# Writing the destination one-hots with the tile index innermost, and loading them with that step

## What is computed

```python
def step(f, _):
    msg = f[src] * edge_weight[:, None]
    agg = jax.ops.segment_sum(msg, dst, num_segments=n)
    f = (1.0 - ALPHA) * agg + ALPHA * feat_0
    return (f, None)
out, _ = jax.lax.scan(step, feat, None, length=K)     # K = 10
```

## Time and profile before

| | us |
|---|---|
| median of 3 runs (8633.08 to 8642.26) | 8638.01 |
| the profiled execution's own span | 8640.6 |
| packing loop, in that span | about 1241 to 1745 |
| the ten hops | about 1750 to 5410 |
| the two single hops | in 7600 to 8640 |

### The profile page before, as it was taken

The page is one execution under the profiler, slowest core; times in us unless marked ns, Lnnn a source line. Parts: engine busy times, 40 slices in busy tenths (PEclk is TensorE's granted clock), DMA queues, the critical chain, the costliest instruction groups (busy, mean ns, idle before and its releaser), DMA issues. The chain is left out here.

```text
span 8640.6 us, 563982 instructions
## 1 busy us (share of the span) xinstructions
PE 7490.3 (87%) x228719; PEld 6386.0 (74%) x228719; DVE 6536.9 (76%) x13039; ACT 4071.0 (47%) x9117; POOL 5548.3 (64%) x5894
## 2 busy tenths in 40 slices
PE   4967758889999999999999999499999899949794
PEld 4856648889999999999999999344444454449794
DVE  5779979978888898888888888544444444478787
ACT  1229969944444444444444444244444444424242
POOL 2520000068888888888888888477777777738384
PEclk7559975589999999999999999799999999979797
DMA  5210026689999999999999999433333333249495
GB/s 80 92 47 0 0 69 246 247 299 342 338 338 339 340 340 336 340 340 338 340 340 338 339 338 339 122 77 79 78 79 79 79 79 77 64 161 339 161 338 166
DMA packets 833483, 1832.18 MB, mean 212 GB/s; under 512 B 245310, under 2 KB 306774, under 8 KB 831838
## 3 DMA queue, kind: packets, MB, share of 16 engines
q1 hardware_dynamic: 752974, 1777.08, 58.4%
q0 software_dynamic: 59776, 46.03, 4.8%
q10 hardware_dynamic: 20624, 7.81, 0.5%
HBM read 1667.67 MB, written 157.79 MB: 211 GB/s over the span
## 5 line engine op out<-in xcount | busy, mean ns | idle before, releaser
L1491 PE MATMUL banks<-arena 128*128 128x48 bf16 x58800 | 2352.6, 184 | 5.4 <-issue 5.4
L1491 PEld LDWEIGHTS banks<-arena 128*128 128x128 fp8e4 x58800 | 2270.5, 95 | 5.9 <-issue 5.7
L1457 DVE TENSOR_TENSOR banks<-banks,wslot 128x384 f32<-128x384 f32 (+1 forms) x3600 | 1984.5, 569 | 343.8 <-PE banks L1491 309.8
L1391 POOL TENSOR_TENSOR arena<-arena 128x768 bf16<-128x768 f32 (+2 forms) x1200 | 1838.3, 1540 | 422.6 <-DVE arena L1461 414.1
L1323 ACT CAST arena<-banks 128x384 bf16<-128x384 f32 (+1 forms) x2400 | 1178.8, 493 | 1872.6 <-DVE banks L1457 1693.7
L1491 PE MATMUL banks<-xc,arena 128*128 128x48 bf16 x24500 | 1943.0, 184 | 62.0 <-DVEq L1470 14.9
L1491 PEld LDWEIGHTS banks<-xc,arena 128*128 128x128 fp8e4 x24500 | 1864.4, 95 | 164.5 <-issue 104.7
L1773 POOL DMA_INDIRECT f<-node_table,idx x1568 | 1554.2, 991 | 557.6 <-issue 466.9
L1461 DVE TENSOR_TENSOR arena<-banks,arena 128x384 f32<-128x384 f32 (+1 forms) x2400 | 1350.4, 574 | 95.4 <-ACT arena L1323 2.3
L1505 PE MATMUL banks<-arena 32*128 32x144 bf16 x80400 | 1374.8, 222 | 21.5 <-issue 13.3
L1505 PEld LDWEIGHTS banks<-arena 32*128 32x128 bf16 x80400 | 1261.2, 93 | 49.2 <-issue 17.8
(11 more groups left out here) (385 smaller groups left out, 13650.6 us busy)
## 6 DMA issues: line engine op xcount, KB each, us to landing
arena<-onehots SPq DMA_DIRECT2D x1200, 512.0 KB, 4.9
arena<-onehots SPq DMA_DIRECT2D x1500, 256.0 KB, 5.2
arena<-onehots SPq DMA_DIRECT2D x300, 576.0 KB, 5.8
arena<-onehots SPq DMA_DIRECT2D x300, 544.0 KB, 5.3
arena<-in_dst SPq DMA_DIRECT2D x195, 512.0 KB
arena<-onehots SPq DMA_DIRECT2D x300, 288.0 KB
onehots<-arena SPq DMA_DIRECT2D x100, 768.0 KB, 3.2
arena<-key_rows SPq DMA_DIRECT2D x196, 196.0 KB
```

What stands on the lines that cost most here:

```text
L1391: nc.gpsimd.tensor_tensor(mp_low[b], mp_rest[b], mp_mid[b], ALU.subtract).then_inc(lo_done[b], 1)
L1457: nc.vector.tensor_tensor(bank, bank, w, ALU.mult).then_inc(m_done, 1)
L1491: m = nc.tensor.matmul(to, g_ring[b][:, i * P:(i + 1) * P], x_part, start=c == 0, stop=c == 2)
```

## The change

The scatter part of all six batches is now made by DVE with the same helper as the source part, so that it stands as `[e, t]`, tiles side by side. ScalarE's Abs and Relu instructions, GpSimd's key copy and their semaphores are gone; ScalarE keeps the fp8 copies. SP sends the same bytes from the same places, in the same order. In the hops the same bytes are loaded, and the ring's scatter part is read as `[e, t]`: a tile's 128 weight columns are 16, 17 or 18 bf16 elements apart (32 to 36 bytes), where they were adjacent.

```diff
-            ACT_B = NBATCH - 1
-            key_now = part(28700, NTILE[ACT_B])
-            far = part(23800, NTILE[ACT_B] * P // 2, BF16)
...
-            def by_tile_outer(to, keys):
-                shape = [P, keys.shape[1], P]
-                return nc.vector.tensor_tensor(to.rearrange("p (t e) -> p t e", e=P), iota_b[:, 0:P].unsqueeze(1).broadcast_to(shape),
-                                               keys.unsqueeze(2).broadcast_to(shape), ALU.is_equal)
-
             def s_part(b):
-                return packed[:, BATCH_AT[b] + G_COLS[b]:BATCH_AT[b] + BATCH_COLS[b]].bitcast(BF16)
+                return packed[:, BATCH_AT[b] + G_COLS[b]:BATCH_AT[b] + BATCH_COLS[b]].bitcast(BF16).rearrange("p (e t) -> p e t", t=NTILE[b])
...
                             by_tile_inner(src_tiles(b), lo_b[:, at]).then_inc(src_hot, 1)
-                            if b != ACT_B:
-                                dve.wait_ge(sent[b], d * 16 + 16)
-                                by_tile_outer(s_part(b), dst_b[:, at]).then_inc(s_hot, 1)
+                            dve.wait_ge(sent[b], d * 16 + 16)
+                            by_tile_inner(s_part(b), dst_b[:, at]).then_inc(s_hot, 1)
...
-                            if b == 0:
-                                act.wait_ge(key_ready, d + 1)
-                                act.sem_inc(sent_seen, 1)
-                            for i in range(b * 3, min(b * 3 + 3, NTILE[ACT_B])):
-                                m = nc.scalar.activation(far[:, i * P:(i + 1) * P], iota_b[:, 0:P], ACT.Abs, bias=key_now[:, i:i + 1], scale=-1.0)
-                            m.then_inc(s_far, 1)
-                        act.wait_ge(s_far, d * NBATCH + NBATCH)
-                        act.sem_inc(sent_seen, 1)
-                        nc.scalar.activation(s_part(ACT_B), far, ACT.Relu, bias=1.0, scale=-1.0).then_inc(s_hot_a, 1)
...
-        s_ring = [part(S_AT[b], S_COLS[b], BF16) for b in range(NBATCH)]
+        s_ring = [part(S_AT[b], S_COLS[b], BF16).rearrange("p (e t) -> p e t", t=NTILE[b]) for b in range(NBATCH)]
...
-                                m = nc.tensor.matmul(banks[:, 4 + q, 0:3 * D], s_ring[b][rows, i * P:(i + 1) * P], mp_b[b][rows, i, :],
+                                m = nc.tensor.matmul(banks[:, 4 + q, 0:3 * D], s_ring[b][rows, :, i], mp_b[b][rows, i, :],
```

More of the change, by code:

```diff
@@ L1084, in place_slots @@
             sent_seen, both_seen = (local(f"pack_{n}") for n in ("sent_seen", "both_seen"))
-            ACT_B = NBATCH - 1
-            ACT_TILES = slice(FIRST_TILE[ACT_B], FIRST_TILE[ACT_B] + NTILE[ACT_B])
-            key_now = part(28700, NTILE[ACT_B])
-            far = part(23800, NTILE[ACT_B] * P // 2, BF16)
-            key_asked, key_ready, s_far, s_hot_a = (local(f"pack_{n}") for n in ("key_asked", "key_ready", "s_far", "s_hot_a"))
             def src_tiles(b):
@@ L1142, in _ @@
                 def _(act):
-                    act.sem_inc(s_hot_a, 1)
                     with act.Fori(0, NGRP) as d:
@@ L1178, in _ @@
                             sp.sem_inc(both_seen, 1)
[L1179 to L1182, removed]
+                            sp.wait_ge(s_hot, d * NBATCH + (b + 1))
                             sp.sem_inc(both_seen, 1)
@@ L1187, in _ @@
                         sp.wait_ge(sent[b], 16 * NGRP + 16)
-            clear([key_asked, key_ready, s_far, s_hot_a, deg_zero, sent_seen, both_seen, src_hot, turned_done, g_kept, s_hot, *sent])
+            clear([deg_zero, sent_seen, both_seen, src_hot, turned_done, g_kept, s_hot, *sent])
             held.close()
@@ L1263, in fetch_scatter @@
                             sp.sem_inc(slot_seen, 1)
-                        sp.dma_start(s_ring[b].bitcast(F32), gs[bass.ds(d * P, P), BATCH_AT[b] + G_COLS[b]:BATCH_AT[b] + BATCH_COLS[b]]).then_inc(s_in[b], 16)
+                        sp.dma_start(part(S_AT[b], S_COLS[b]), gs[bass.ds(d * P, P), BATCH_AT[b] + G_COLS[b]:BATCH_AT[b] + BATCH_COLS[b]]).then_inc(s_in[b], 16)
                     def turn(g, d, before):
```

## The result

| | before | after |
|---|---|---|
| median, us (11 runs each, timed together) | 8638.75 | 8655.13 |
| lowest to highest, us | 8629.45 to 8643.33 | 8645.27 to 8661.95 |
| span of the profiled execution, us | 8640.6 | 8654.5 |
| a group in the packing, us | 19.7 | 17.86 |
| a group in the hops, us | 14.347 | 14.614 |

The ratio after to before is 1.0018, 95% interval 1.0010 to 1.0027. The forecast was 8570, with a range up to 8645: both the size and the sign were wrong.

The account below looks back on a forecast made before the run. ScalarE was taken to bound the packing, with VectorE close behind, and TensorE the hops. 8640.6 - 85 (packing) + 15 (hops) = 8571, so 8570 us for the median; eight in ten within 8550 to 8645.

Parts of the forecast that it names:

- What bounded what: Before the change: ScalarE sets the packing's pace, VectorE a few per cent behind; TensorE has no slack in the hops.
- one nanosecond on a quad is 30 us: Hops: 29,700 quads run on a TensorE without slack, so each nanosecond more on a quad costs 30 us.
- The new form's price on VectorE: Packing: the tile-inner form of the destination part takes VectorE 1.27 us for 16 tiles, instead of 2.28.
- The packing, 16.46 us a group: Packing after the change: TensorE's batches sum to 16.46 us a group and bound it, down from 19.8, VectorE at 16.0.
- ScalarE's sum: Packing: ScalarE keeps only its copies, 1.99 us for a batch of 16, about 12.1 us a group.
- 4 us to spare against TensorE: Packing: ScalarE's 12.1 us a group leave it 4 us below TensorE's 16.46.
- the 85 that the packing was to give: Packing's gain: 24 groups x (19.8 - 16.46) = 80 us, and 5 us at the ends.
- The first quad of each stretch: Hops: its stepped load is uncovered, 900 stretches at 17 to 47 ns more, 15 to 42 us; 15 taken.
- rival 1: Hops: the stepped load keeps its 60 ns at 2.4 GHz but stays hidden; 8598 us, chance 20%.
- Covered at either end, narrowly at the upper one: Hops: a quad's 60 to 63 ns of moving columns hide a stepped load of 30 to 60 ns.
- rival 2: Hops: stepped load keeps 60 ns and doesn't fit; 1.5 ns a quad gives the gain back, 4 ns makes 8717; 12%.
- rival 5: Packing: gives only half, as the write-back or three-way hand-over of buffers costs extra; 8613 us, chance 9%.

Follow-up runs that it names:

- run 7: Changed kernel with one tiny ScalarE copy ahead of the packing loop, so the activation table loads there: 8625.79 against 8641.65 us, ratio 0.9981.
- run 3: Changed kernel with 48 instead of 144 moving columns in every scatter matmul but the first of each group: 8577.5 us, one run.
- run 5: Changed kernel with 48 moving columns in the scatters and weight steps of 4 to 30 bytes in batches 0 to 5: 8550.09 us, one run.
- Run 8: Changed kernel, table load out of the loop, batches 0, 2 and 4 copied to adjacent columns by GpSimd or ScalarE: 8699.26 against 8641.65 us, ratio 1.0064.
- run 6: Changed kernel fetching the scatter part whole only for each hop's first two groups, then 64 bytes a partition: 8650.43 us, one run.
- run 9: Changed kernel, table load ahead of the loop, scatter part's tiles innermost in groups of four: 8582.38 against 8635.93 us, ratio 0.9936.
- run 11: Changed kernel, table load still in the loop, batches of 18, 18, 14, 18, 14 and 17 tiles: 8606.52 against 8635.93 us, ratio 0.9965.
- run 12: Changed kernel with run 11's batches, scatter part in fours in batches 0, 2 and 4 alone, table load out of the loop: 8600.14 against 8637.67 us, ratio 0.9957.
- run 10: Kernel of run 9 with the source part in groups of four tiles too: 8623.09 against 8635.93 us (kernel before), ratio 0.9987.

## Why the prediction was wrong

**What bounded what: right.** ScalarE was the packing's limit, VectorE next; and "one nanosecond on a quad is 30 us" in the hops is what decided.

**The new form's price on VectorE: right**, 1288 ns where 1.27 us was said.

**The packing, 16.46 us a group: wrong, by a table load.** The failed step is ScalarE's sum, "so about 6.1 x 1.99 = 12.1 us a group", and under it the statement ahead of the prediction that the table load in the loop was gone with Abs and Relu. It was not: before and after have 25 of them, 1283 ns each. The sum put it at nothing, and the "4 us to spare against TensorE" were taken over the whole group, while what counts is the one batch behind the load. Before, the load was a part of the pace that ScalarE set anyway; after, it stands ahead of batch 0's copies with TensorE behind them. The shortened list of instructions shows the row for before and not for after, and that was read as an absence. Price: 16.57 us a group without it, 17.86 with it, 25 x 1.29 = 32 us; run 7 gives the same, 0.9981 against 1.0018 is 32 us, and 53.4 + 32 is the 85 that the packing was to give. With it out, TensorE's sum of 16.46 held within 0.11 us. So rival 5, whose packing gave half for other reasons (the write-back, the hand-over of buffers), falls: at 16.57 us a group TensorE waits for nothing.

**The first quad of each stretch: right in mechanism, wrong in size.** The term was 15 us, with 42 as the other end: "I take the clock's end, 15 us, by the nearest rows at both levels". Those rows were fp32 loads of adjacent columns, and a step is another limit: 60 ns at 1.2 GHz and 60 to 62 at 2.4 (runs 3 and 5). Measured: 45 ns, 900 times, 41 us, rival 1's price. Run 8 took the step away from just these loads and got the 73 ns back.

**"Covered at either end, narrowly at the upper one": wrong in part.** It was covered, and too narrowly. Against 62.4 ns of cover a load of 60 to 62 is no margin, and long quads, nearly all of them in the batches with a step of 32 bytes, cost 0.151 us a group, 1.5 ns a quad: rival 2, at the point from which it was said to decide. 0.151 x 300 = 45 us. Its mechanism isn't settled. Shown is that it isn't the DMA's traffic (run 6), that nearly all of it goes with the 32-byte step (runs 9 and 11) and that with 48 moving columns no quad but the first of a stretch has a median over 66 ns (run 3). Why loads of 60 ns with a step of 28 bytes lengthen nothing isn't shown. That the reads of weights and of moving data meet at that step is only argued.

0.135 + 0.151 is 0.286 us a group against 0.267 measured; the pause before the third stretch is 0.02 shorter. 0.267 x 300 = 80, and the hops took 70 more in the profiled executions. Most of the other 10 lies where one hop meets the next: from the start of a hop's last group to that of the next hop's first, and from there to its second, the time changed by -0.05 and -0.15 us in the mean of the ten hops, and not by +0.27.

**Put together**: forecast 8571; the table load adds 32, the load's price 26, the long quads 45: 8674; less 16 by the last paragraph (0.019 x 300 = 6, and 10) and 3 elsewhere it is 8655, against 8654.5. All three misses point the same way. Rival 2 joined the last two, with 12% for all its sizes; the table load had no chance at all, and no rival joined a packing that gives less to hops that cost more.

## What to carry to other kernels

Weights that are loaded with a step of 16 bytes or more cost by the lines that they touch, and the clock doesn't help: 60 ns at both levels here. Keep two entries within 16 bytes. Putting the innermost loop of a one-hot on four tiles instead of all keeps most of the fast write's speed and of the load's: ratio 0.9936 against 0.9981, both with the table load out of the loop, or 39 us. Where a cost is "just hidden", subtract the cover from the cost at its upper end, and ask what happens at the first instruction of each stretch, or after a signal that comes late (run 12), which has no cover. Before saying that an instruction has left a loop, look up every row of the loop: here the table load followed the activations that stay. And look at the granted clock of the stretch before a gain is put down to the edit (run 11).

## What the runs showed of the hardware that wasn't expected

- A quad's weight loads of 128 bf16 entries at 2.4 GHz: hidden in 25 to 34 ns up to a step of 8 bytes (some 17 ns above adjacent ones where bare, run 9), 47 at 12, 60 to 62 from 16 to 36 (runs 3 and 5). At 1.2 GHz: 27 adjacent, 33 at 8 bytes (run 10), 60 to 62 at 32 to 36.
- Under 144 moving columns, three to five of 16 quads with a 32-byte step take 65 to 70 ns in the median; with 34 bytes it is two of 17 at about 65, with 36 at most one of 18, with 28 none (kernel after and run 11).
- ScalarE's copy of 2048 bf16 out of a stepped view takes 4.14 us.
- VectorE's compare with runs of four takes 1.34 to 1.42 or 1.75 us for 16 tiles, by the group, where runs of 16 take 1.29.
- A table load (1283 ns) stays in a loop whose activations are all the same copy; one such activation ahead of the loop takes it out (run 7).
- TensorE's granted clock in the packing is 0.50 in the kernels before and after and in runs 7 and 9; between 1300 and 1650 us it is 0.61 in run 11, 0.55 in run 10 and 0.52 in run 12.
